# Making the next turn's first attention stacks at the end of the turn before, in a tower kernel on Trainium2

## What is computed

```python
def tok(x, w_qkv, b_qkv, w_out, b_out):              # attention, 16 heads of 16 channels
    q, k, v = split(x @ w_qkv.T + b_qkv)
    attn = softmax(q @ k.T / sqrt(16))
    return (attn @ v) @ w_out.T + b_out

h = tok(x)                                            # 512 tokens
h = concatenate([cls_tok, h])                         # 513 tokens
h = h + scan_block(layernorm(h))                      # gated linear scan
h = h + bit_ffn_conv(layernorm(h))                    # quantised, 256 -> 1024 -> 256, with a convolution
h = h + state_space(layernorm(h))                     # 512 channels, 16 states
h = h + bit_glu(layernorm(h))                         # quantised gate, up and down projections
```

## Time and profile before

| | |
|---|---|
| median of 3 runs | 2540.73 us (2538.59 to 2546.09) |
| the profiled execution's own time | 2544.26 us |
| its span (first to last instruction) | 2542.4 us |
| TensorE busy | 2142.9 us, 84% |
| VectorE busy | 2029.6 us, 80% |
| ScalarE busy | 1488.5 us, 59% |
| GpSimd busy | 1120.8 us, 44% |
| chain of waits, shares | VectorE 40%, TensorE 39%, ScalarE 9%, issue 8%, GpSimd 3%, DMA 1% |

### The profile page before, as it was taken

How to read it: one execution, slowest core, us unless ns; L and a number is a source line. 1 busy time by engine, 2 the same in 40 slices (tenths; PEclk the granted TensorE clock), 3 DMA queues, 4 the chain that set the end, 5 groups by cost and what they waited for, 6 DMA issues and landing times.

```text
span 2542.4 us, 26885 instructions
## 1 busy us (share of the span) xinstructions
PE 2142.9 (84%) x9366; PEld 1193.9 (47%) x9366; DVE 2029.6 (80%) x2434; ACT 1488.5 (59%) x2363; POOL 1120.8 (44%) x562
## 2 busy tenths in 40 slices
PE   3998878897799887989779898788978988878897
PEld 1326664345423765434542476543553246644445
DVE  6865879997785588998788477999788747799977
ACT  2654468765275447875537544787453644577744
POOL 1220249982222115997222111799522311279952
PEclk8999999999899998999899998899989999889998
DMA  6200000000220000000031000000003100000000
GB/s 202 84 6 1 1 1 1 1 1 1 83 77 1 1 1 0 1 1 1 1 109 51 1 1 1 1 0 1 1 13 112 36 1 1 1 1 0 1 1 17
DMA packets 41087, 51.45 MB, mean 20 GB/s; under 512 B 9072, under 2 KB 32368, under 8 KB 40944
## 3 DMA queue, kind: packets, MB, share of 16 engines
q1 hardware_dynamic: 40944, 49.62, 6.3%
HBM read 26.25 MB, written 10.49 MB: 14 GB/s over the span
## 4 chain that ended last, share of the span: by engine, by line
DVE 40%; PE 39%; ACT 9%; issue 8%; POOL 3%; DMA 1%; SPq 1%; DVEq 0%; ACTq 0%; POOLq 0%
DVE big L1983 16%; PE psum L755 11%; PE psum L902 5%; ACT big L1197 4%; PE psum L818 3%; ACT mid L1197 3%; PE psum L890 3%; PE psum L875 3%; PE psum L1057 3%; DVE big L1652 2%; PE psum L1089 2%; POOL big L2132 2%; DVE mid L1596 2%; DVE negmax L1704 2%; DVE mid L1524 2%
## 5 line engine op out<-in xcount | busy, mean ns | idle before, releaser
L1197 ACT ACTIVATE big<-psum 128x512 f32<-128x512 f32 (+2 forms) x604 | 455.8, 774 | 277.3 <-PE psum L890 146.8
L2132 POOL TENSOR_TENSOR big<-big 128x2048 f32<-128x2048 f32 x124 | 561.8, 4530 | 41.3 <-DVE big L1983 41.2
L1057 PE MATMUL psum<-big,ident 128*128 128x512 f32 x992 | 507.0, 617 | 65.6 <-POOL big L2132 65.6
L1983 DVE TENSOR_TENSOR_SCAN big<-psum,b,big 128x512 f32<-128x512 f32 x404 | 490.2, 1265 | 6.9 <-ACT psum L1197 6.6
L1704 DVE TENSOR_REDUCE negmax<-psum 128x1 f32<-128x512 f32 x512 | 318.7, 678 | 47.2 <-PE psum L875 46.1
L1197 ACT ACTIVATE psum<-mid,aneg 128x512 f32<-128x512 f32 x404 | 268.5, 680 | 80.2 <-DVE big L1983 80.1
L1057 PEld LDWEIGHTS psum<-big,ident 128*128 128x128 f32 x992 | 174.4, 193 | 230.9 <-POOL big L2132 141.3
L875 PE MATMUL psum<-mid 96*128 96x512 bf16 x512 | 189.0, 389 | 49.3 <-DMA mid<-mid 38.1
L890 PE MATMUL psum<-mid 98*128 98x512 bf16 x512 | 182.2, 382 | 20.1 <-ACT big L1197 14.3
L1197 ACT ACTIVATE mid<-mid 128x513 f32<-128x513 f32 (+3 forms) x120 | 104.3, 883 | 154.7 <-DVE mid L1993 80.6
L2096 POOL TENSOR_TENSOR big<-big,mid 128x513 f32<-128x513 f32 x40 | 50.8, 1282 | 286.3 <-ACT big L1197 286.3
(11 more groups left out here) (224 smaller groups left out, 3837.5 us busy)
## 6 DMA issues: line engine op xcount, KB each, us to landing
mid<-mid SPq DMA_DIRECT2D x192, 64.0 KB, 2.6
mid<-scratch SPq DMA_DIRECT2D x192, 64.0 KB, 2.2
scratch<-big SPq DMA_DIRECT2D x4, 1536.0 KB, 6.1
out<-hres SPq DMA_DIRECT2D x8, 513.0 KB, 5.0
big<-in_x SPq DMA_DIRECT2D x8, 512.0 KB, 5.5
big<-in_w SPq DMA_DIRECT2D x2, 1024.0 KB, 6.4
big<-in_wg SPq DMA_DIRECT2D x1, 1024.0 KB, 9.7
big<-in_wu SPq DMA_DIRECT2D x1, 1024.0 KB, 11.6
```

Of the source, the lines that this page charges most:

```text
L1057: mm = nc.tensor.matmul(y_psum[:, c], ident[:, :], st(1, k)[:, c], start=(n == 0), stop=(n == NS - 1))
L1197: return nc.scalar.activation(o, a, func, **kw)
L1983: V.tensor_tensor_scan(st(0, k)[:, c], decays(DT * k + c), bx, b0[:, p, n, c:c + 1], ALU.mult, ALU.add).then_inc(scanned, 1)
L2132: G.tensor_tensor(st(1, k), st(0, k), c_row(k).unsqueeze(1).broadcast_to([P, DT, S]), ALU.mult).then_inc(hc_ready, 1)
```

## The change

q and k of the next turn's batch 0, their parts and the stacks of its first four heads are made at the end of each turn. The products are `products_ahead` in two pairs, `next_heads(0)` and `next_heads(1)`, one ahead of the transposes of batch 1's maxima and one ahead of its token rows; the fillers at these places are gone. In the last turn one product that nobody reads stands in for each pair. ScalarE makes the high parts ahead of `copy_rows(3, (1,))` and the middle parts around `round_last(3, 1)` (for batch 0 this was VectorE's work). VectorE makes the rests ahead of `scale_tiles(3, 1)`, two low parts ahead of `round_tiles(3, 1)` and two between the additions of batch 0 and batch 1. The DMA queue waits for the parts, copies the first group's twelve and waits for their landing before it stores the turn's outputs. At the next turn's start it copies the remaining groups, 24 copies right away and 12 after the first maxima. TensorE has no wait ahead of the first head's scores but `turn_start`.

The inputs come into the tile `onorm`, which attention's outputs use later, and are loaded once the convolution's block is through. The parts of batch 0 lie in `big` now, where the exponentials of the third head are written; so ScalarE waits there for all four groups' copies. Ahead of the first turn the same work (`at_first`) stands between the setup's conversions, and `turn_start` is raised after it. VectorE's loop runs three times, with the last turn as straight code behind it.

The diff, cut to its core:

```diff
-WARM = {"affine": 20, "T0": 12, "I1_0": 10, "T1_1": 14, "I1_1": 6, "LN3": 8, "T2": 4, "T3_1": 14, "I3_1": 6}
+WARM = {"affine": 20, "T0": 12, "I1_0": 10, "T1_1": 14, "I1_1": 6, "LN3": 8, "T2": 4}
...
+    order.extend([("n0", 0), ("T3", 1), ("n1", 0), ("I3", 1), None, ("S3", 1), None, ("y0", 0), None, ("y1", 0), None, None,
+                  ("y0", 1), None, ("y1", 1)])
...
+        rest0 = [osb[:, :], lsum[:, :]] + [big[:, W8 + 1 + n * S:W8 + 1 + (n + 1) * S] for n in range(2)]
...
+                 for t, o in ((big, W8 + 1 + 2 * S), (big, 2 * W8))]
+        xin = onorm[:, :, :].rearrange("p (b k) q -> p b k q", b=PAIR)
...
+            def stack_first(sems):
+                for part, made in enumerate((sems.high, sems.mid, sems.low)):
+                    for of in range(2):
+                        sp.wait_ge(made, of + 1)
+                        stack_part(0, part, sems.stacked, of)
+                sp.wait_ge(sems.stacked, 12 * 16)
+            stack_first(at_first)
+            sp.nop().then_inc(turn_start, 1)
...
-                for j in range(NG - 1):
-                    stack_heads(j)
+                for j in range(1, NG - 1):
+                    stack_rest(j)
...
-                    sp.wait_ge(q_ready, 4 * PAIR)
-                    sp.wait_ge(q_first, 2 * PAIR)
+                    sp.wait_ge(f_silu, HT * PAIR)
                     for p in range(PAIR):
                         load_x(i + 1, p)
+                    stack_first(ahead)
...
+                next_heads(0)
                 token_maxima(3, (1,))
+                next_heads(1)
                 token_rows(3, (1,))
                 down_project(1, "y", wd)
...
             with pe.Fori(0, TURNS - 1) as i:
-                turn_products(i)
-                first_products(i + 1)
-            turn_products(TURNS - 1)
+                turn_products(i, False)
+            turn_products(TURNS - 1, True)
...
                     act.wait_ge(st_full, v + 1)
+                    if v == 4:
+                        for j in range(1, NG):
+                            act.wait_ge(stacked0[j], 12 * 16)
...
                 round_last(3, 0)
+                if not last:
+                    load_ln_exp()
+                    act.wait_ge(q_scaled, q_of(3, 0))
+                    act.wait_ge(pool_scaled, PAIR + 1)
+                    for k in range(4):
+                        high_ahead(ahead, k)
                 copy_rows(3, (1,))
+                if not last:
+                    for k in range(2):
+                        mid_ahead(ahead, k)
                 round_last(3, 1)
+                if not last:
+                    for k in range(2, 4):
+                        mid_ahead(ahead, k)
...
                 round_tiles(3, 0)
+                if not last:
+                    for k in range(4):
+                        rest_ahead(ahead, k)
                 scale_tiles(3, 1)
+                if not last:
+                    for k in range(2):
+                        low_ahead(ahead, k)
                 round_tiles(3, 1)
-                add_ffn(1, "y")
+                add_ffn(1, "y", (0,))
+                if not last:
+                    for k in range(2, 4):
+                        low_ahead(ahead, k)
+                add_ffn(1, "y", (1,))
```

234 lines of the change are left out of this document (136 added, 98 removed).

## The result

The changed kernel takes 2507.9 us (median of 4 runs, 2505.78 to 2509.93) against 2541.45 us for the kernel before in the same comparison. The ratio is 0.987, with a 95% interval of 0.9854 to 0.9886. The forecast was 2499 us, with a range of 2489 to 2512 us. The profiled execution took 2506.92 us, with a span of 2505.1 us (before: 2544.26 and 2542.4). One execution of the seventh experiment's kernel took 8525.97 us at a granted clock of 0.226; it is left out of that kernel's median and ratio.

A forecast was written before the change was run, and what follows sets the result against it. The chain of waits at turn seams A (659 us), B (1285), C (1910) bounds it. -39.8 + 2.3 - 5.4 + 9.6 + 0 - 8.5 = -41.8 us from median 2540.73 gives 2499 us; range 2489 to 2512.

The forecast's parts named there:

- The wait that goes: At the three seams between turns, waiting for products, splits and copies ahead of the first scores disappears: -39.8 us.
- the first turn: After the setup, scores start about 40.5 + 0.7 instead of 49.73 us: -8.5 us, bounds 6 and 10.
- The restart: Loop branches right ahead of the scores, no longer hidden: 1.0 us at two seams, 0.3 at the last, +2.3 us.
- Rival (b): Branches cost the whole 2.7 us at the two seams where the loop turns: 2502.4 us, chance 0.1.
- The first step: First head's step after each seam takes 3.1 us with TensorE's clock kept: 1.8 us saved at each, -5.4 us.
- The turn's end: Work added at three turn ends, partly covered, costs 3.0, 3.3 and 3.3 us: +9.6 us, bounds 0 and 20.
- The last turn's end: Fourth turn's end without fillers: token rows 1.7 us later, projection 1.6 back, 0 in sum, bounds -2 and +2.
- The DMA queue: In the new turn, copies for heads 4 to 7 covered by 2.8 us, the exponentials' new wait by over 4.
- (c): Copies for heads 4 to 7 collide with the store of batch 1's output: 2506 us, chance 0.1.
- (e): DMA queue bounds attention's start, copies taking 1.10 us instead of 0.67: slower, 2549 us, chance 0.05.
- Rival (a): TensorE's clock not kept: slow second eight passes at two turn ends, first step 4.6 to 5.2: 2509 us, chance 0.15.
- Rival (d): Work at the turns' ends is fully covered, 9.6 us less: 2489 us, chance 0.1.

The follow-up runs named there:

- seventh experiment: Changed kernel with the four rests behind VectorE's scaling of batch 1's tiles instead of ahead of it: 2510.06 us, ratio 0.9859.
- third experiment: Changed kernel with both TensorE's and VectorE's loops written out as straight code: 2507.61 us, ratio 0.9856.
- fifth kernel: Changed kernel with TensorE's and VectorE's loops written out and the first two low parts behind the rounding: 2499.71 us, ratio 0.9806.
- first experiment: Changed kernel with only TensorE's loop written out as straight code, other engines keeping their loops: 2515.77 us, ratio 0.9892.
- last experiment: Changed kernel, both loops written out, low parts behind rounding, fillers ahead of second projections and inside turns (not gated block's ten), last turn's fillers back: 2475.6 us, ratio 0.9741.

## Why the prediction was right, and where it wasn't, step by step

The time came out inside the range, and the mechanism, the copies' wait gone from the seams, is what the trace shows. Two terms were mis-sized, and both in the same direction.

**The wait that goes: right.** The chain has no landing of a copy at any seam, and nothing else waits there. In the first turn the scores start at 39.10 instead of 49.73 us, 10.6 us earlier, beyond the upper bound of 10; the first step there took 1.0 us more (5.37 against 4.34), which leaves 9.6 where 8.5 was forecast.

**The restart, +2.3 us: this step failed.** It cost 3.2 us at A, 3.0 at B and 0.0 at C (from the last addition to the first score, less the 1.3 and 1.2 us that the kernel before took from there to its first products); 6.2 in all. The place was right, the loop's branch and not C. What failed is the value of 1.0, and even the bound of 2.7 us above it: that was read from another engine, VectorE's idle time of 4.04 less the 1.3 us in which the semaphores are cleared. The subtraction was wrong too, since VectorE's stall lies beside that clearing and not behind it. And a branch could be seen by itself: in the trace of the kernel before, VectorE's (`L1569`) ends at 658.13 us and VectorE's next instruction starts at 661.45, 3.32 us later. TensorE stood idle 4.68 and 4.40 us around its own branch, against 1.42 in straight code, so it pays 3.3 and 3.0 us beyond the clearing. Rival (b), the whole bound, was the nearer one. The rule of the Trainium skill (Runtime: NRT & Kernel Launch, section on instruction fetch mechanics), that a taken branch to a page that isn't there must fetch it first, agrees with the trace: 3.49 and 3.21 us at taken branches, each with a 16 KB transfer of instructions in it, and 0.24 without one at the straight place. I had read it and gone by less.

**The first step, -5.4 us: half right.** It gave 1.0 at A, nothing at B (0.6 lost) and 1.9 at C: -2.3 us. The step rested on "a gap of some 2 us". Where the gap was 1.4 to 1.7 us (C, and all seams of the third experiment) the step took 3.1 us as forecast; where the branch made it 4.4 to 4.7 us, the clock had fallen. With both branches taken out and nothing else changed, the steps at A and B fell by 1.1 and 2.1 us, so there this miss is the restart's miss once more: a stall costs its length and then TensorE's clock behind it. But a short gap isn't enough. The fifth kernel's three steps took 4.4 to 4.6 us behind gaps of 1.4 to 1.8 us, and C took 4.76 behind 1.43 when the changed kernel ran again. Leaving out the two steps of the first experiment that wait for VectorE, the last projection ahead had taken 5.0 to 5.6 us wherever the step behind so short a gap took 4.1 to 4.8 us, and 5.8 to 6.6 us wherever it took 3.1. So at C the term of 1.8 us held partly by luck: the forecast looked only at the gap, and the clock's low stretch had fallen into the projection instead (granted 0.55 over C's projection, 0.72 over B's).

**The turn's end, +9.6 us: right in sum, less so by seam.** From the first scaling to the last addition it grew by 2.2, 2.8 and 4.3 us, 9.3 in all, where 3.0, 3.3 and 3.3 were forecast. The rests cost 0.4 us thanks to the cover, shown by the seventh experiment. The last projection starts 17.02 us after the first scaling at B, against 15.53 before (+1.5; forecast +1.7), and from there to the last addition it takes 1.3 more (forecast 1.6). At A the collision that was forecast didn't come: TensorE idled 0.86 us ahead of the transposes instead of 3.40, and the clock held (granted 1.00 over 634 to 643 us). The added products are only a small part of that, 3.76 us for the fillers' 3.18; most is that the token rows ahead had taken 5.08 us instead of 2.83. At C the projection lost more than forecast (6.49 us for 32 passes, against 3.68 before). That the two nearly cancel is luck.

**The last turn's end, 0: right.** It gained 0.9 us. The kernel before, with TensorE's loop written out, had 25.5 us there, so 0.9 is within what executions differ by. With the 20 fillers put back, in the last experiment, it was 25.4 us, against 25.0 and 25.9 without them: what they give at the token rows is lost again at the projection.

**The DMA queue: right.** Steps of heads 4 to 7 stand 3.1 us apart with no gap on a copy, and the first exponentials come 28.6 us after the first score (687.14 - 658.58), where it was 29.6.

```profile
687.14 10.70 ACT L1248 ACTIVATE big<-psum 128x1024 f32<-128x1024 f32 x11 [10.31 <-PE psum L938]
```

ScalarE's idle time there is 10.31 us, 10.32 before. Rivals (c) and (e) fall. Rival (a), whose 2509 us is the number nearest to the measured one, came true in a half: the first step's clock fell at A and B, but the second eight passes kept theirs; what made up the number was rival (b)'s branch. Rival (d) falls with the 9.3 us.

**The sum.** 3.9 us from the restart and 3.1 from the first step, less 0.3 at the end's work, make 6.7 at the seams; 1.1 more than forecast at the start, and 1.2 from inner stretches and the end, give 37.3 instead of 41.8 (rounding leaves 0.1). The other half of the miss against 2499 us lies outside the change. The profiled execution of before stood 2.8 us above its median and that of after 1.0 below, so the medians lie 33.55 us apart. What single executions of one kernel differ by is not shown: the two traces of the changed kernel are 1.1 us apart, and only 0.1 of it lies in the inner stretches.

**What the prediction didn't have:** that an inner stretch isn't a constant. It set those four at 0, and in the changed kernel that came out (-0.3 us), but not for a reason that it gave. With the seams 1.0 to 10.1 us shorter the same code took between 7.5 us less and 7.8 us more. What stays open is what decides how long TensorE's clock stays low behind a given gap. The runs show that it varies from turn to turn of one kernel, that an edit which moved each seam by 0.5 to 0.7 us changed it, and that it doesn't vary where the gap is filled.

## What to carry to other kernels

Before taking work out of a seam, ask what else it hid: here a loop's taken branch cost TensorE and VectorE about 3 us as soon as nothing lay beside it, and at two seams TensorE's clock behind it too. The engines' stalls lie beside each other, so taking out one alone gave 1.0 us at the seams and both together 7.6. When a gain at one place doesn't appear in the time, cut both traces at fixed marks and look for stretches of unchanged code that changed their length; here short gaps in TensorE's work made them swing by 10 us, and unread products in those gaps won 12 us (2487.7 to 2475.6). A filler belongs where TensorE only waits; ten of them in front of a product that others wait for cost about 2 us a turn.

## What the runs showed of the hardware that I hadn't expected

A taken loop branch stalled TensorE 3.0 and 3.3 us beyond straight code (2.5 to 3.4 over the five traces that keep the loop), and stands in VectorE's chain with 3.03 us; the two lie beside each other. Forty fp32 matmuls of one shape took 5.65 us at a granted clock of 1.00, between 6.74 and 8.51 in four turns of the changed kernel, and up to 9.95 at 0.52 in the kernel before, with the same code there. A kernel with two added reductions per seam, its seams 1.8 us longer in sum, ran 9.8 us faster than the one without.
